# Cross-attention and quantised FFN, 16 batches: another order for the setup work of the first two batches

## What is computed

```python
def xattn(x, y, ...):                      # x is layer-normed before
    y_dca, y_main = y[:, -16:, :], y[:, :-16, :]
    kv_dca = (y_dca @ Wkv_dca + bkv_dca).reshape(b, 16, 2, H, HD)   # H = 16, HD = 32
    k_dca, v_dca = ln(kv_dca[:, :, 0], kn_dca_w, kn_dca_b), kv_dca[:, :, 1]
    q = ln((x @ Wq + bq).reshape(b, s1, H, HD), qn_w, qn_b)
    kv = concat(y_main @ Wk + bk, y_main @ Wv + bv)    # interleaved by head
    k, v = ln(kv[..., :HD], kn_w, kn_b), kv[..., HD:]
    ctx = softmax(q k^T * scale) v + softmax(q k_dca^T * scale) v_dca
    return ctx @ Wo + bo
def ffn(x, kernel, bias):                  # x is layer-normed before
    y = relu(fq(x, 8, -1) @ fq(kernel, 8, 0) + fq(bias, 8, -1))     # fq: fake quantisation, 8 bits
    return fq(y, 8, -1)
x = x + xattn(layernorm(x), ctx, ...);  x = x + ffn(layernorm(x), ...)
```

## Time and profile before

| | |
|---|---|
| time, median of 3 runs | 365.11 us (364.85 to 365.71) |
| the profiled execution, its own time | 362.07 us |
| its span | 360.2 us |
| busy: PE, DVE, ACT, POOL | 313.4 us (87%), 312.0 (87%), 222.2 (62%), 173.7 (48%) |
| chain that ended last, by engine | PE 70%, issue 3%, DVE 3%, DMA 2%, ACT 1% |

### The profile page before, as it was taken

How to read it: one execution, slowest core, us unless ns; L and a number is a source line. 1 busy time by engine, 2 the same in 40 slices (tenths; PEclk the granted TensorE clock), 3 DMA queues, 4 the chain that set the end, 5 groups by cost and what they waited for, 6 DMA issues and landing times.

```text
span 360.2 us, 7522 instructions
## 1 busy us (share of the span) xinstructions
PE 313.4 (87%) x2321; PEld 251.0 (70%) x2321; DVE 312.0 (87%) x804; ACT 222.2 (62%) x444; POOL 173.7 (48%) x261
## 2 busy tenths in 40 slices
PE   0499789799999899999999999999999999787732
PEld 0336547678888788887878787878888888586520
DVE  2977999999989899999998989998999999966564
ACT  3347987465666667676767676767585856453400
POOL 5201423337372828282828282828282827272620
PEclk9999999999999999999999999999999999989985
DMA  7980187727170909191929191819191909080002
GB/s 244 266 298 1 54 153 130 141 52 143 44 151 16 203 28 174 46 177 45 159 63 167 52 169 46 174 47 174 50 171 52 170 12 164 18 148 0 31 0 87
DMA packets 36451, 38.88 MB, mean 108 GB/s; under 512 B 8760, under 2 KB 27452, under 8 KB 36412
## 3 DMA queue, kind: packets, MB, share of 16 engines
q1 hardware_dynamic: 36044, 38.14, 49.9%
q10 hardware_dynamic: 368, 0.27, 0.3%
HBM read 16.89 MB, written 4.72 MB: 60 GB/s over the span
## 4 chain that ended last, share of the span: by engine, by line
PE 70%; issue 3%; DVE 3%; DMA 2%; ACT 1%; SPq 1%; POOL 0%; ACTq 0%; DVEq 0%
PE bank L1330 34%; PE bank L1447 13%; PE bank L1416 4%; PE bank L1594 4%; PE bank L1427 3%; PE bank L1428 3%; PE bank L1604 2%; PE bank L1501 2%; PE bank L1466 2%; DMA k_stack<-k_lo 2%; PE bank L1496 2%; PE bank L1564 1%; SPq L377 1%; DVE finals L1051 1%; ACT prob_store L750 1%
## 5 line engine op out<-in xcount | busy, mean ns | idle before, releaser
L1447 PE MATMUL bank<-v_aug,prob_store 128*128 128x66 f32 x512 | 68.2, 277 | 3.4 <-ACT prob_store L750 3.4
L517 POOL TENSOR_TENSOR k_lo<-wkv_raw,k_hi 128x448 f16<-128x448 f32 x16 | 16.8, 1047 | 107.0 <-issue 99.1
L1447 PEld LDWEIGHTS bank<-v_aug,prob_store 128*128 128x128 f32 x512 | 64.0, 194 | 5.6 <-ACT prob_store L750 4.4
L1062 DVE TENSOR_REDUCE neg_max<-bank 128x4 f32<-128x448 f32 (+1 forms) x128 | 45.2, 416 | 5.8 <-PE bank L1416 5.4
L761 ACT ACTIVATE wkv_raw<-bank,affine 128x448 f32<-128x448 f32 (+1 forms) x32 | 22.4, 749 | 39.6 <-PE bank L1496 39.3
L750 ACT ACTIVATE prob_store<-bank,exp_scale 128x512 f32<-128x512 f32 x64 | 41.6, 677 | 6.4 <-PE bank L1428 6.4
L536 POOL TENSOR_TENSOR finals<-seg_out 128x128 f32<-128x128 f32 x64 | 34.4, 546 | 13.0 <-DVE seg_out L1075 12.9
L1427 PE MATMUL bank<-q_stack,k_stack 128*128 128x128 f16 x256 | 34.7, 222 | 1.9 <-ACT maxT L612 1.9
L1428 PE MATMUL bank<-maxT,sel 128*128 128x128 bf16 x256 | 34.5, 222 | 0.0
L1427 PEld LDWEIGHTS bank<-q_stack,k_stack 128*128 128x128 f16 x256 | 26.8, 106 | 6.1 <-issue 3.9
L1075 DVE TENSOR_TENSOR seg_out<-bank,rden 128x256 f32<-128x256 f32 x64 | 27.2, 424 | 3.8 <-POOL finals L536 1.4
(11 more groups left out here) (211 smaller groups left out, 860.8 us busy)
## 6 DMA issues: line engine op xcount, KB each, us to landing
x_in<-in_x SPq DMA_DIRECT2D x16, 256.0 KB, 3.1
q_stack<-q_hi SPq DMA_DIRECT2D x32, 128.0 KB, 3.8
q_stack<-q_lo SPq DMA_DIRECT2D x32, 128.0 KB, 4.8
...
```

Source lines behind the costliest of these rows:

```text
L1062: v.tensor_reduce(neg_max[:, HG * gr:HG * (gr + 1), seg], s4[:, :, lo:hi], AX.X, ALU.max, negate=True).then_inc(max_ready.sem, 1)
L1447: last = mm(bank[6 + gr % 2][:, VW * h:VW * (h + 1)], probs[:, gr % 2, h], v_aug[:, Bt.parity, HG * gr + h], start=True, stop=True)
```

## The change

It is an order change. The number of instructions on each engine stays the same up to how they are grouped; none is made longer or shorter, and SP and GpSimd keep their order.

```diff
--- before.py
+++ after.py
@@ -636,22 +636,23 @@
...
 
+            def setup_selectors():
+                act.wait_ge(rows_selected.sem, 1)
+                for seg, lo, hi in ((0, 0, MAIN), (1, MAIN, P)):
+                    copy(sel[:, :, lo:hi], sel_rows[:].rearrange("p (h s) -> p h s", s=2)[:, :, seg:seg + 1]
+                         .to_broadcast([P, H, hi - lo])).then_inc(sel_made.sem, 1)
+
...
                 setup_transposed()
+                setup_selectors()
...
 
-            def setup_selectors():
-                act.wait_ge(rows_selected.sem, 1)
-                for seg, lo, hi in ((0, 0, MAIN), (1, MAIN, P)):
-                    copy(sel[:, :, lo:hi], sel_rows[:].rearrange("p (h s) -> p h s", s=2)[:, :, seg:seg + 1]
-                         .to_broadcast([P, H, hi - lo])).then_inc(sel_made.sem, 1)
-
@@ -662,17 +663,18 @@
...
 
+            def setup_copied(j):
+                act.wait_ge(kvdca_ready.sem, j + 1)
+                copy(kv_dca[:, j, 0], bank[4 + j][:, :]).then_inc(kvdca_copied.sem, 1)
+
             def setup_squares():
-                for j in range(2):
-                    act.wait_ge(kvdca_ready.sem, j + 1)
-                    copy(kv_dca[:, j, 0], bank[4 + j][:, :]).then_inc(kvdca_copied.sem, 1)
+                setup_copied(1)
...
 
-            def setup_values():
-                for j in range(2):
-                    act.wait_ge(kvdca_ready.sem, j + 3)
-                    copy(kv_dca[:, j, 1], bank[7 - j][:, :]).then_inc(kvdca_copied.sem, 1)
+            def setup_values(j):
+                act.wait_ge(kvdca_ready.sem, j + 3)
+                copy(kv_dca[:, j, 1], bank[7 - j][:, :]).then_inc(kvdca_copied.sem, 1)
@@ -771,6 +773,7 @@
...
                     if N.first():
+                        setup_squares()
@@ -790,12 +793,17 @@
...
                 if N is not None:
+                    normed(kT_ready, 6, MAIN, 2, k_n, kn_ready, klo_ready)
                     if N.first():
-                        setup_dca(0)
-                    normed(kT_ready, 6, MAIN, 2, k_n, kn_ready, klo_ready)
+                        setup_heads()
...
                     high(q_hi, q_n, qn_ready, P, qstack_in, qhi_ready)
+                    if N.first():
+                        setup_dca(0)
+                        setup_values(0)
+                        setup_columns()
+                        setup_values(1)
@@ -808,11 +816,9 @@
...
                             copy(bias_full[:, n], made[:, :]).then_inc(bias_copied.sem, 1)
-                        setup_squares()
+                        setup_copied(0)
...
                         token_statistics()
-                        setup_columns()
-                        setup_heads()
@@ -844,9 +850,7 @@
...
                     setup_wo()
-                    setup_values()
                     setup_ffn()
-                    setup_selectors()
@@ -1161,12 +1165,10 @@
...
                     if N.first():
-                        setup_scales()
-                        setup_dca(0)
+                        setup_affine()
...
                     if N.first():
-                        setup_dca(1)
-                        setup_pairs()
+                        setup_squares()
@@ -1192,10 +1194,11 @@
...
                         low_queries()
+                        biased_keys()
                         setup_norms()
-                        setup_affine()
-                        biased_keys()
-                        setup_squares()
+                    elif N.first():
+                        setup_scales()
+                        setup_dca(0)
@@ -1246,8 +1249,9 @@
...
                     if N.first():
+                        setup_dca(1)
+                        setup_pairs()
                         biased_keys()
-                        setup_output()
@@ -1296,6 +1300,7 @@
...
                         head_products(A)
+                        setup_output()
@@ -1343,23 +1348,22 @@
...
 
-            def setup_keys():
+            def setup_keys(j):
...
                 pe.wait_ge(wd_centred.sem, 1)
-                for j in range(2):
-                    for c in range(YC):
-                        mm(bank[4 + j][:, :], y_dcaT[:, j, c, :], wd_raw[:, c, 0, :], start=c == 0, stop=False)
-                    mm(bank[4 + j][:, :], ones3[0:3, :], bias_split[:, 2], start=False, stop=True).then_inc(kvdca_ready.sem, 1)
-
-            def setup_values():
-                pe.wait_ge(out_bias_ready.sem, 1)
-                for j in range(2):
-                    if j:
-                        pe.wait_ge(*kn_ready.of(Batch(0)))
-                    for c in range(YC):
-                        last = mm(bank[7 - j][:, :], y_dcaT[:, j, c, :], wd_raw[:, c, 1, :], start=c == 0, stop=c == YC - 1)
-                    last.then_inc(kvdca_ready.sem, 1)
+                for c in range(YC):
+                    mm(bank[4 + j][:, :], y_dcaT[:, j, c, :], wd_raw[:, c, 0, :], start=c == 0, stop=False)
+                mm(bank[4 + j][:, :], ones3[0:3, :], bias_split[:, 2], start=False, stop=True).then_inc(kvdca_ready.sem, 1)
+
+            def setup_values(j):
+                if j:
+                    pe.wait_ge(*kn_ready.of(Batch(0)))
+                else:
+                    pe.wait_ge(bias_copied.sem, 2)
+                for c in range(YC):
+                    last = mm(bank[7 - j][:, :], y_dcaT[:, j, c, :], wd_raw[:, c, 1, :], start=c == 0, stop=c == YC - 1)
+                last.then_inc(kvdca_ready.sem, 1)
@@ -1397,7 +1401,7 @@
...
                 pe.wait_ge(wo_in.sem, 16)
-                pe.wait_ge(bias_copied.sem, 2)
+                pe.wait_ge(kvdca_copied.sem, 3)
@@ -1451,8 +1455,6 @@
...
                         pe.wait_ge(sel_made.sem, 2)
-                if N is not None and N.first():
-                    setup_output()
@@ -1490,7 +1492,8 @@
...
                         pe.wait_ge(bv_sum_ready.sem, 1)
-                        setup_dca(0)
+                    if N.second():
+                        pe.wait_ge(kvdca_copied.sem, 4)
@@ -1518,8 +1521,10 @@
...
                         setup_biases()
-                        setup_keys()
-                        setup_columns()
+                        setup_keys(0)
+                    elif N.first():
+                        setup_dca(0)
+                        setup_values(1)
@@ -1545,10 +1550,13 @@
...
                                   ).then_inc(q_ready.sem, 1)
+                    if A.first():
+                        setup_keys(1)
+                        setup_columns()
                 if N is not None and N.first():
+                    setup_dca(1)
+                    setup_output()
                     setup_columns_wide()
-                    setup_values()
-                    setup_scales()
@@ -1610,6 +1618,8 @@
...
                                   ).then_inc(v_ready.sem, 1)
+                if N is not None and N.first():
+                    setup_scales()
```

## The result

The changed kernel took 366.43 us (median of 22 runs, 363.35 to 368.98), the kernel before beside it 365.90 us (22 runs, 362.10 to 367.98); ratio 1.0053, 95% interval 1.0027 to 1.0078. The forecast was 366.8 us, slower. In the means the first comparison is +0.6 us and a second one (e10) -0.2 us, with twice the standard error at 1.0 and 1.4.

What follows compares the result with a forecast made beforehand. The prediction took ACT up to 45.7, DVE up to 67, then PE as bounds in turn. Its terms, -4.8 + 0.9 + 5.3 + 0.3 - 0.9 + 0.9 = +1.7, on 365.11 gave 366.8 us, range 364.5 to 368.0.

Steps and rivals of the forecast that it cites:

- Step 1: Batch 0's q product earlier on PE: scaling of k on DVE starts at 31.6 instead of 36.42, -4.8 us.
- Step 2: ACT's DCA scale work and its wait for DVE's reduction ahead of q_hi: q_hi at 36.5, +0.9 us.
- Step 3: ACT between q_hi and batch 1's squares: 3.4 us of inserted work plus 1.9 of waits, +5.3 us.
- Step 4: DVE from sums to maxima: out_bias now directly ahead of the maxima, +0.3 us; moved selectors cost 0.
- Step 5: DVE against POOL: DVE comes later, k_low is over, only POOL's sum still holds the split, -0.9 us.
- rival b: POOL's operations slip with DVE and collide as much as before: 367.7 us, chance 0.12.
- Step 6: PE's clock falls near 54, slowing k and q products that the weighting waits for, +0.9 us.
- Rival a: PE's clock holds: only +0.8 us, 365.9 us, chance 0.28.
- Rival c: Faster: waits on ACT before batch 1's squares don't arise, squares before 45.0; -1.1 us, 364.0 us, chance 0.15.

Runs made afterwards that it cites:

- e10: The changed kernel run again, nothing altered: 364.80 us, ratio 0.9965 to the kernel before.
- e2: Changed kernel with ACT's Ln and Exp of the DCA scale moved back behind q_hi: 366.14 us, ratio 1.0020 to the kernel before.
- e3: Changed kernel with ACT's token statistics of batch 2 moved behind the squares of batch 1: 363.10 us, ratio 0.9941 to the kernel before.
- e9: The kernel before compared with itself, nothing altered: 366.73 us, ratio 1.0054.
- e12: Changed kernel with columns and second DCA transposes earlier on PE, two absolute values later on ACT, POOL's first residual sum later: 363.86 us, ratio 0.9961.
- e1: Kernel before with only the selectors moved ahead of the weights' copies on ACT: 363.13 us, ratio 0.9943 to the kernel before.
- e5: Changed kernel with only the selectors put back behind the FFN scales on ACT: 365.61 us, ratio 1.0015 to the kernel before.
- e4: Changed kernel with the gain columns on PE ahead of the second DCA key product: 363.26 us, ratio 0.9956 to the kernel before.
- e7: Changed kernel with six spare matmuls on PE ahead of batch 0's q product: 364.43 us, ratio 1.0012 to the kernel before.
- e6: Changed kernel with POOL's first residual sum moved behind the four combinations: 364.89 us, ratio 1.0042 to the kernel before.
- e8: Changed kernel with five moves at once on PE, ACT and DVE, including late token statistics and earlier output bias: 366.49 us, ratio 1.0081.

## Why the prediction was right, and where not

The value, +1.7, was met by +1.65 at the context transposes in the first profile, by +0.6 between the second profiles, and by +0.5 in the medians; terms that were wrong both ways cancel. That 366.43 us lies so near to 366.8 is luck in part: the kernel before, forecast from its 365.11, had a median of 365.90 in the comparison, 0.8 higher, and only the other 0.5 is the difference between the kernels.

- *Step 1, -4.8:* mis-sized. It was -4.2 in the profile (32.26 against 36.42), -3.0 between the second profiles (31.39, 34.40). I had let the q product follow the key product at once, at 23.84. With a quick key product it is released by DVE's low part of the query weights, at 22.99, 2.00 us after PE was free. So a quick first key product, which gives the kernel before 2.0 us at the scaling (34.40 against 36.42), gives the changed kernel 1 (30.43 and 30.46 in e2 and e3 against 31.39 in e10, where it was slow). Then the clock was 0.57 over 24 to 28, with matmuls of 0.63 instead of 0.39: the q product took 4.33 us (22.99 to 27.32) against 2.90 in e3 at the full clock and 3.2 in my sum. The earlier start and the slower pace nearly cancel: it ended 0.3 later than the 27.0 of my sum, and the key product and the columns behind it took another 0.3 more than I had given them (27.32 to 31.04, 3.7 us instead of 3.4). A fall of the clock such as I looked for at 54 cost here as well.
- *Step 2, +0.9:* right. `q_hi` 4.82 after the scaling, 3.95 before: +0.87, with the wait for `dca_small` (0.67).
- *Step 3, +5.3:* right. From `q_hi` to the squares 10.14 us against 4.69: +5.45, and 10.13 in e10 against 4.69 in e9. The waits are 1.43 (1.3 foreseen), 0.27 (0.4) and none (0.2). e12 takes two of the inserted pieces out, e3 another piece of the same queue, and in both the gain arrives.
- *Step 4, +0.3:* sums to maxima 5.65 against 5.49, +0.16; right. That the selectors cost nothing was wrong, as the next point shows: PE was indeed ahead of DVE, but POOL behind PE was not harmless.
- *Step 5, -0.9:* size nearly right (7.77 against 8.38, -0.6), reason wrong. POOL's two operations did not stay behind while DVE slipped; they slipped by 1.50 (`k_low` 57.10 to 58.60), as rival b had it. That the hold of 1.1 us on `wo_lo` still went is due to the selectors (e1, e5). What remains is 0.30 on the CAST and 1.04 on the split, and 0.6 of that is the clock's doing: with the clock up, in e4, the stretch took 7.19 us. So this step by itself was -1.2, and +0.6 of the measured sum belongs to the next.
- *Step 6, +0.9:* near in size, wrong in its path. The clock fell to 0.50 at about 55 and was back at 58. I had let PE's products of k and q be slow and hold the weighting; in this profile they were hardly touched (two matmuls of k, at 57.34 and 57.88), and from `k_raw` to the context transposes it is 5.30 us as in the kernel before. The fall cost 0.6 us all the same, by another way: it slowed the transposes for the norms, by these POOL's two operations, and by these DVE (e4). In e10 and e7 the clock stayed at 0.50 until past 59; there the foreseen path adds 0.35 us (5.66 and 5.63 instead of 5.30), together 0.9. From the last maxima to the context transposes it is 13.07 us in the changed kernel, 13.42 and 13.38 in e10 and e7, and 12.49 in e4, where the clock held; with POOL's sum late it is 12.60 in e6, with the fall, and 11.74 in e12 without.

Against the forecast, steps 1 and 3 came 0.6 and 0.15 dearer, steps 4, 5 and 6 0.15, 0.3 and 0.3 cheaper. That this sums to nothing is luck. Rival a, the clock that holds, is what e4 shows: 0.6 us cheaper, not 0.9.

Rival c needed the squares before 45.0: 47.22 and 46.37 were measured, and as long as ACT's queue ahead of them was the changed one, never less than 45.51 (e4). The error in the time itself is larger than these terms: the period near the end took 3.1 us more in one profile of the kernel before than in another, with the clock at 0.50 instead of 0.95.

On the holds: the CAST at 59.20 ends when `k_low` does (59.68 and 59.64), the split at 59.72 when the sum does (60.95 and 60.89). The split has two inputs in SBUF, and the rule of the Trainium skill, "SBUF — State Buffer", section "Who interferes with whom", covers it; e6 confirms it, 0.19 without the sum. The CAST has one input, and in e4 one took 0.93 us and ended with the sum (58.41 and 58.37). The page has such an instruction held only in a mode that uses both ports; whether this one runs in that mode no row shows. POOL is held as well: its sum takes 1.27 to 1.30 us, but took 1.85 in the kernel before and 1.75 in e5 and e8, each time when `q_lo` ran on DVE at its start. In e9, where the two start together, it is `q_lo` that took 1.83 instead of 0.68.
